# An attention block with Q and K projected transposed, V projected in one pass, and the sums turned through DRAM

## What is computed

```python
q = (X @ Wq), k = (X @ Wk), v = (X @ Wv)         # 16, 8, 8 heads of 64
q = q * cos + rotate_half(q) * sin; k likewise
att = 50 * tanh(q @ k.T / 16 / 50); causal; softmax
y = att @ v                                       # heads side by side, 1024 columns
x = layernorm(X + y @ Wo)
q8, s = int8 per token of x; ffn = (q8 @ weight.T) * s * w_scale + bias, to float16
out = layernorm(x + ffn)
```

## Time and profile before

| | us |
|---|---|
| median of 3 runs (1562.66 to 1565.54) | 1562.99 |
| span of the profiled execution | 1559.7 |
| start to the first score | 54.8 |
| a pair of attention | 36.1 |
| last weighing of a batch to the next tanh | 91.4 |
| TensorE, DVE, ACT, POOL busy | 1415.9, 1272.7, 986.5, 546.2 |

### The profile page before, as it was taken

How to read it: one execution, slowest core, us unless ns; L and a number is a source line. 1 busy time by engine, 2 the same in 40 slices (tenths; PEclk the granted TensorE clock), 3 DMA queues, 4 the chain that set the end, 5 groups by cost and what they waited for, 6 DMA issues and landing times.

```text
span 1559.7 us, 26316 instructions
## 1 busy us (share of the span) xinstructions
PE 1415.9 (91%) x8576; PEld 1141.8 (73%) x8576; DVE 1272.7 (82%) x3228; ACT 986.5 (63%) x1374; POOL 546.2 (35%) x529
## 2 busy tenths in 40 slices
PE   3699999989789999998969999998997999999894
PEld 3588878757678887866768788885776888888572
DVE  7888888867878888885788888887678888888575
ACT  5577777763367777784337777777335777777632
POOL 2433333333323333332433333333242333333434
PEclk9899999999989999999989999999999999999997
DMA  7300000311100000032110000002210000000211
GB/s 236 129 1 1 1 1 1 109 63 52 49 9 1 1 1 1 1 108 75 44 53 1 1 1 1 1 1 108 81 53 36 1 1 1 1 1 1 108 55 41
DMA packets 25337, 55.98 MB, mean 36 GB/s; under 512 B 3824, under 2 KB 12528, under 8 KB 23920
## 3 DMA queue, kind: packets, MB, share of 16 engines
q1 hardware_dynamic: 20592, 45.88, 8.6%
q10 hardware_dynamic: 4608, 8.39, 1.4%
...
## 4 chain that ended last, share of the span: by engine, by line
PE 58%; issue 12%; DVE 12%; ACT 11%; POOL 6%; DMA 0%; ACTq 0%; POOLq 0%; DVEq 0%; SPq 0%
PE ps L516 19%; PE ps L460 16%; PE ps L492 13%; PE ps L559 4%; ACT qkT L664 4%; ACT probs L677 4%; PE ps L526 3%; ACT sums L693 2%; POOL rstd L1048 1%; POOL f L1056 1%; DVE qkT L834 1%; DVE stats L938 1%; PE ps L476 1%; PE ps L477 1%; POOL prob_lo L1039 1%
## 5 line engine op out<-in xcount | busy, mean ns | idle before, releaser
L1039 POOL TENSOR_TENSOR prob_lo<-probs,prob_hi 128x1024 fp32r<-128x1024 f32 x128 | 310.8, 2428 | 559.6 <-DVE prob_hi L848 559.6
L460 PE MATMUL ps<-w_split,xT 128*128 128x256 f32 x3072 | 420.4, 288 | 30.2 <-DVE xT L788 22.3
L460 PEld LDWEIGHTS ps<-w_split,xT 128*128 128x128 f32 x3072 | 404.9, 195 | 48.1 <-issue 22.3
L516 PE MATMUL ps<-prob_hi,v 128*65 128x512 f32 (+3 forms) x1280 | 425.1, 381 | 13.8 <-POOL prob_lo L1039 12.0
L677 ACT ACTIVATE probs<-ps 128x1024 f32<-128x1024 f32 x288 | 295.4, 1026 | 160.9 <-PE ps L492 152.9
L492 PE MATMUL ps<-qkT 128*128 128x512 f32 (+1 forms) x1280 | 322.0, 378 | 14.9 <-DVE qkT L834 14.9
L683 ACT ACTIVATE probs<-probs 128x1024 f32<-128x1024 f32 x288 | 305.5, 1061 | 8.8
L492 PEld LDWEIGHTS ps<-qkT 128*128 128x128 f32 x1280 | 229.3, 193 | 73.8 <-DVE qkT L834 16.1
L664 ACT ACTIVATE qkT<-ps 64x256 fp32r<-64x256 f32 x512 | 193.5, 378 | 106.9 <-PE ps L477 101.6
L848 DVE CAST prob_hi<-probs 128x1024 fp32r<-128x1024 f32 x288 | 203.2, 706 | 54.1 <-POOL probs L1031 26.1
L834 DVE TENSOR_TENSOR qkT<-ps,qkT 64x256 fp32r<-64x256 f32 x512 | 215.1, 420 | 35.0 <-ACT qkT L664 26.8
...
## 6 DMA issues: line engine op xcount, KB each, us to landing
wo<-wo_split SPq DMA_DIRECT2D x8, 2048.0 KB, 7.5
...
x_in<-X SPq DMA_DIRECT2D x32, 256.0 KB, 3.1
result<-probs ACTq DMA_DIRECT2D x32, 256.0 KB, 2.0
wo_split<-y SPq DMA_DIRECT2D x2, 2048.0 KB, 7.3
...
y<-L_attn_Wo SPq DMA_DIRECT2D x1, 2048.0 KB, 10.4
y<-L_attn_Wk SPq DMA_DIRECT2D x4, 256.0 KB, 6.8
```

Of the source, the lines that this page charges most:

```text
L460: mm = nc.tensor.matmul(ps[:, proj_bank(j, t), 0:QKV], xT[:, a, k, rows], w_split[:, w, k, j, :], start=(k == 0 and a == w == 0), stop=(k ...
L516: mm = nc.tensor.matmul(sums_ps[:, :, GQ - n:GQ], v[:, j % 2, kt, w0:w1], p[:, g % ring, col:col + REP * n].rearrange("p (h q) -> p h q", ...
L1039: nc.gpsimd.tensor_tensor(prob_lo[:, g % PRING, :], probs[:, g % PRING, :], prob_hi[:, g % 2, :].bitcast(F32), ALU.subtract).then_inc(low_ ...
```

## The change

- **Units.** Four units of two pairs per batch (U = 16 in all, number m) take the place of pairs for the projection. Weights now stand on TensorE and tokens stream: a chunk is 128 output channels of all heads in a unit by up to 1024 columns, 24 matmuls of 512 columns. Unit m has chunk 0 (K, both halves of the tokens) and chunks 1 and 2 (Q, one half of the tokens each). They come out transposed, so `turn_qk`, `round_qk` and `split_qk` go. While unit m - 1 is in attention (18 steps), chunk 0 is projected in its steps 0 to 2, chunk 1 in 5 to 7, chunk 2 in 9 to 11, 8 matmuls each step. Also unit 0 of the next batch is projected beside the last unit of this one. The last unit of all has nothing beside it.
- **Rope.** Output channels are ordered so that the halves that rope exchanges lie in other partitions or columns. `rope_read` (DVE, out of PSUM, three passes for K, two for Q), `rotate` (POOL, adds and subtracts 1024 columns), `round_rope` (ACT) and `rope_low` (DVE) follow. SP puts the parts from the tile `work` to `qk` by DMA inside SBUF, 8 DMAs per chunk and part, 48 per unit.
- **V.** `project_v` makes V of all heads, 12 matmuls of 512 columns per token tile, once per batch; `round_v` (ACT) and `split_v` (DVE) split it. Tiles 0 to 4 come around the last two weighings of the batch before, 5 to 7 behind project_out(0).
- **Weights.** They are split at the start, unit by unit, by ACT and DVE or POOL in four stages that lie in other tiles, stored to DRAM (w_scratch) and loaded again for each unit. The rope tables are spread and turned once.
- **Sums.** `put_sums` stores unscaled sums (64 rows, rows of 512 B) and divisors of each group to DRAM in turned order, three DMAs. At the end of a batch the divisors are loaded into `div`, inverted, stored; ACT's queue loads them broadcast (`load_rb`, two DMAs per tile, one buffer), SP loads y; `scale_y` on POOL multiplies, `round_y` (ACT) and `split_y` (DVE) split. `turn_sums`, `finish_group` and `turn_y` go.
- **Order.** The loop over batches is unrolled in the program. The tail of the row phase stands alone before the next batch's scores.

The core of the diff (declarations, start and counts of semaphores are left out):

```diff
+                for i in range(2):
+                    if x == 0:
+                        for half in range(2):
+                            src = work_r[64 * half + 32 * i:64 * half + 32 * (i + 1), 0, 1 - low, :].bitcast(F32)
+                            for copy in range(2):
+                                r0 = 64 * copy + 32 * half
+                                sp.dma_start(buf[r0:r0 + 32, i, 2 + low, :].bitcast(F32), src
+                                             ).then_inc(k_put[m % 2][i], 16)
...
+                        for r in range(REP):
+                            h = REP * i + r
+                            for half in range(2):
+                                src = work_r[32 * h:32 * (h + 1), x, 1 - low, half * HT:(half + 1) * HT].bitcast(F32)
+                                r0 = 64 * low + 32 * half
+                                sp.dma_start(buf[r0:r0 + 32, i, r, cols].bitcast(F32), src
+                                             ).then_inc(q_put[m % 2][x - 1][i], 16)
...
+                for h in range(REP):
+                    sp.dma_start(y_scratch[2 * c:2 * c + 2, h * HD:(h + 1) * HD, j, :].rearrange("t d n -> d t n"),
+                                 sums[0:HD, slot, h * GQ:(h + 1) * GQ].rearrange("d (t n) -> d t n", t=2)
+                                 ).then_inc(sums_put[slot], 16)
+                sp.dma_start(d_scratch[2 * c:2 * c + 2, :, j, :].rearrange("t h n -> h t n").unsqueeze(0),
+                             sums[HD:HD + 1, slot, :].rearrange("a (h t n) -> a h t n", h=REP, t=2)
+                             ).then_inc(sums_put[slot], 16)
...
+                for slot in range(2):
+                    sp.wait_ge(sums_put[slot], sums_put_upto(b))
+                sp.dma_start(div[:, :], d_scratch.rearrange("t h j n -> (t h j) n")).then_inc(div_loaded, 16)
+                for x in range(1, 3):
+                    wait_put(sp, min(UB * b + UB, U - 1), x)
+                for t in range(YRING):
+                    load_y(b, t)
+                for t in range(XRING):
                     load_x(b, t)
...
+                sp.wait_ge(div_done, b + 1)
+                sp.dma_start(r_scratch.rearrange("t h j n -> (t h j) n"), div[:, :]).then_inc(div_stored, 16)
...
+                products = [(n, k, w, a) for n in range(2) for k in range(KC) for w, a in ((0, 0), (0, 1), (1, 0))]
+                for n, k, w, a in products[lo:hi]:
+                    half, slot = (n, 0) if x == 0 else (x - 1, 1 + n)
+                    mm = nc.tensor.matmul(ps[:, bank + n, :], w_ring[:, slot, w, k, :],
+                                          xT[:, a, k, half * HT:(half + 1) * HT],
+                                          start=(k == w == a == 0), stop=(k == KC - 1 and w == 1))
+                if hi == len(products):
+                    mm.then_inc(projected, 1)
...
+                        score(b, g)
+                        if m is not None:
+                            for x, at in enumerate((0, 5, 9)):
+                                if at <= s < at + 3:
+                                    project(m, x, 8 * (s - at), 8 * (s - at) + 8)
+                        if g >= 2:
+                            weigh(b, g - 2)
+                if more:
+                    project_v(b + 1, 0)
+                weigh(b, NB - 2)
+                if more:
+                    project_v(b + 1, 1)
+                weigh(b, NB - 1)
+                if more:
+                    for t in (2, 3, 4):
+                        project_v(b + 1, t)
+                for t in range(NT):
+                    if t == 1 and more:
+                        for n in (5, 6, 7):
+                            project_v(b + 1, n)
...
+            def load_rb(b, t):
+                if t == 0:
+                    act.wait_ge(div_stored, 16 * (b + 1))
+                    wait_put(act, min(UB * b + UB, U - 1), 0)
                 else:
...
+                    act.wait_ge(y_scaled, rows_upto(b, t - 1))
+                for h in range(REP):
+                    act.dma_start(rb[h * HD:(h + 1) * HD, :, :].rearrange("p k n -> p (k n)"),
+                                  r_scratch[t, h].rearrange("k n -> (k n)").partition_broadcast(HD)
+                                  ).then_inc(rb_loaded, 16)
...
+            def round_y(b, t):
+                act.wait_ge(y_scaled, rows_upto(b, t))
+                if t >= 2:
+                    act.wait_ge(o_done, rows_upto(b, t - 2))
+                elif t == 0:
+                    wait_put(act, min(UB * b + UB, U - 1), 1)
+                nc.scalar.activation(y_hi[:, t % 2, :, :], y_raw[:, t % YRING, :, :], ACT.Copy).then_inc(y_hi_done, 1)
...
+                        if m is not None and s in (5, 10, 14):
+                            round_rope(m, (5, 10, 14).index(s))
                         cap(b, g)
...
+                load_rb(b, 0)
+                load_rb(b, 1)
+                round_y(b, 0)
+                load_rb(b, 2)
+                round_y(b, 1)
+                if more:
+                    for t in range(5, NT):
+                        round_v(b + 1, t)
                 for t in range(1, NT):
+                    if t + 2 < NT:
+                        load_rb(b, t + 2)
                     if t + 1 < NT:
...
+                        round_y(b, t + 1)
...
+                if x == 0:
+                    cos_k, sin_k = (table[:, :].rearrange("p (a c) -> p a c", a=2) for table in (cosT, sinT))
+                    nc.vector.tensor_tensor(turned, halves, cos_k, ALU.mult)
+                    nc.vector.scalar_tensor_tensor(out=crossed[0:HD], in0=halves[HD:P], scalar=-1.0, in1=sin_k[0:HD],
+                                                   op0=ALU.mult, op1=ALU.mult)
+                    nc.vector.tensor_tensor(crossed[HD:P], halves[0:HD], sin_k[HD:P], ALU.mult).then_inc(proj_read, 1)
+                else:
+                    cols = slice((x - 1) * HT, x * HT)
+                    swapped = bass.AP(tensor=halves.tensor, offset=halves.offset + 512,
+                                      ap=[[8 * 512, P], [-512, 2], [1, 512]])
+                    cos_q, sin_q = (table[:, cols].unsqueeze(1).broadcast_to([P, 2, HT]) for table in (cosT, sinT))
+                    nc.vector.tensor_tensor(turned, halves, cos_q, ALU.mult)
+                    nc.vector.tensor_tensor(crossed, swapped, sin_q, ALU.mult).then_inc(proj_read, 1)
+            def rope_low(m, x):
+                dve.wait_ge(rope_hi, chunks_upto(m, x))
+                nc.vector.tensor_tensor(work_r[:, x, 0, :], work[:, x, 0, :], work_r[:, x, 1, :].bitcast(F32),
...
+                        if m is not None and s in (3, 8, 12):
+                            rope_read(m, (3, 8, 12).index(s))
+                        if g >= 1:
+                            probs_of(b, g - 1)
+                        if m is not None and s in (6, 11, 15):
+                            rope_low(m, (6, 11, 15).index(s))
...
+            def rotate(m, x):
+                pool.wait_ge(proj_read, chunks_upto(m, x))
+                pool.sem_inc(wait_passed, 1)
+                if x == 0:
+                    nc.gpsimd.tensor_tensor(work[:, 0, 0, :], work[:, 0, 0, :], work[:, 0, 1, :],
+                                            ALU.add).then_inc(rotated, 1)
...
+                        mask(b, g)
+                        if m is not None and s in (4, 9, 13):
+                            rotate(m, (4, 9, 13).index(s))
...
+            def scale_y(b, t):
+                pool.wait_ge(y_loaded[t % YRING], ring_upto(b, t, YRING))
+                pool.wait_ge(rb_loaded, 32 * rows_upto(b, t))
+                nc.gpsimd.tensor_tensor(y_raw[:, t % YRING, :, :], y_raw[:, t % YRING, :, :], rb[:, :, :],
+                                        ALU.mult).then_inc(y_scaled, 1)
...
+                scale_y(b, 0)
+                scale_y(b, 1)
+                for t in range(1, NT):
+                    inverse_std(b, t - 1, 0, mv1, veps1, rstd1, z_done)
+                    if t + 1 < NT:
+                        scale_y(b, t + 1)
```

1121 lines of the change are left out of this document (632 added, 489 removed).

## The result

The changed kernel takes 1832.71 us (median of 4, 1830.25 to 1833.75) beside 1562.83 for the kernel before on the same chip: a ratio of 1.172, 95% interval 1.171 to 1.174, slower by 17%. The prediction was 1661 with a range of 1575 to 1720: the direction was right, the size far outside.

A forecast was written before the change was run, and what follows sets the result against it. Attention was taken as TensorE-bound. Start 78, attention 279.8 + 2 x 274.8 + 250, handoffs 3 x 125.5 and end 124 gave a span of 1658 us, 1661 as run; range 1575 to 1720.

The forecast's parts named there:

- the chain: Attention, score to weighing on the other engines: 4.5 to 5.7 us a group against TensorE's 4.6, with rope passes queued ahead.
- The first rival: Attention: TensorE paces the units, 59 us each, since engine queues recover within a unit; 1541 us in all; 12 in 100.
- where projection products follow they cover the delay: stalls 1.1 us at step 4, 0.5 at step 7: Attention unit: products in steps 5 to 7 and 9 to 11 hide rope delays; only the third chunk lacks cover, 3.9 us.
- the size of rotate: POOL's rope additions and subtractions in attention: 2.43 us per chunk, like a low part, three times per unit.
- the collision of POOL and DVE: Attention: each of three rotates can hold DVE, a cast taking 1.82 us instead of 0.7; adds 2.4 us a unit.
- The split of x: End of a batch's attention: falls into the bare steps of unit 2 and costs 3.5 us.
- SP has room: SP's queue in attention: 48 puts at some 0.35 us, 17 of 67 us per unit, and 8 more for sums.
- The third rival: Attention and handoff: puts and broadcasts land late, 2 us more a unit and 6 a handoff, 1715 us; 17 in 100.
- Handoff: Last weighing to next batch: sums through DRAM in series, project_out(0) at 18.8 us, next score at 125.5; 105 lost over three.
- SP issues five loads meanwhile: Handoff: five loads issued during the 0.5 us reciprocal, given no cost of their own; the store after it 2.4 us.
- The loop of 12.9: Row phase: period rises from 8.46 to 12.9 us through scale_y, two issues, round_y, keep_q and norm1, less split_y.
- The start: Before the first score: weight loads, splits, stores, K rope and puts; first score at 78 us, 23 lost, bounds 68 and 92.

## Why the prediction was right or wrong

**Right: that the direction is decided by the chain, not by TensorE.** Without its waits TensorE needs some 61 of the second unit's 72.7 us (forecast 59), and the unit didn't follow. The first rival (60.5 or less a unit) fell: even without rotate a unit takes 61 to 65.

**Wrong: "where projection products follow they cover the delay: stalls 1.1 us at step 4, 0.5 at step 7".** This is the step that failed: in the unit shown above the waits outside the third chunk are 7.3 us, not 1.6. Two things were missing in it. I had ACT waiting for rotate ahead of the tanh at the third chunk only, where I counted 3.9 and 4.35 came. The same order acts at all three chunks, with 3.5 to 5.8 us of standstill on ACT each, and the products of one step (8 times 0.234, 1.9 us) don't cover that. Moving the rounding alone gave back 74 us; attention was under-forecast by 114. And the size of rotate: 2.43 was taken from a low part, but for Q it is two passes that DVE's casts and low parts interrupt, 3.5 us in the mean (1769 and 1730 ns). One pass gave back 19. How far the two gains overlap was not tried. With rotate away altogether attention takes 1072 us in sum over the batches, where 1075 was forecast with it: the forecast fits a kernel without rotate.

**Mis-sized: the collision of POOL and DVE.** The prediction had the row, a cast of 1.82, and priced it at 2.4 a unit, then took 67 because terms overlap. Casts take up to 2.89 and rose by 444 ns in the mean, which is 8 us over the 18 casts of a unit, not all of it on the path. The Trainium skill, SBUF — State Buffer, Who interferes with whom, has the shared port pair as an exclusive lock: the engine that issues first holds it for its whole instruction, and the other is blocked. The rows of split_y (3.29 beside a pass of 2.40 that began 0.20 before) agree with this; in the units, where both engines keep issuing, POOL's passes get longer too (1.27 to 2.26 for 512 columns).

**Third unit.** The split of x was put at 3.5 and cost 4.7: the third unit takes 78.5 with it and 73.8 in batch 3, which has none. ACT waits for its load (16.1 us in all, 36.3 with the rounding moved), and the load goes out 13 us behind the end of the projection, since it stands behind the puts of chunk 1. A term of transfer was missing; I had costed only the engines' passes.

**Right in part: the puts.** TensorE's waits for Q and K's puts are 28.8 us: 26.0 ahead of the first score, 2.9 in the first unit and none later, so the puts themselves land in time. But they cost SP 0.62 each, not 0.35, and "SP has room" left out what stands behind them: the load of x in each third unit, and the first score. The third rival, late puts, has next to nothing for it in attention; in the handoff it was partly true.

**Handoff: 126.5 against 140.** Of the 13.4 us, 4.4 come before the first projection: the store of the reciprocals takes 6.0 instead of the 2.4 taken from the result's store at 2.0. It is issued right behind three loads of y and two of x, which the working passed over with "SP issues five loads meanwhile"; no run takes these loads away, so that they are what delays it is likely, not shown. Another 1.5 come until residual1(1) ends (46.4 against 40.5), the rows give 6.6 (76.8 against 70.2; 3.7 of it at tile 2, 14.8 where 11.1 was forecast, and 11.6 with the weights late and V first) and the tail 1. The Trainium skill, DMA: Bandwidth & Descriptors, Anatomy of one DMA, has about 2.0 us fixed a transfer; its section is written for transfers that GpSimd issues, and all of these are issued by SP or ACT. The divisors' load at 1.7 and the puts at 2.0 to 2.3 are near it all the same; the store at 6.0 and the broadcasts at 4.0 are not, and the measurement decides.

**Rows: mechanism right, another loop longer.** The loop of 12.9 exists: the run with keep_q first has it at 12.9 to 13.3. I wrote that TensorE's own work falls and "so it waits", and didn't ask what it waits for: keep_q behind round_y, and residual1 behind TensorE at its lower clock. That loop is 13.7 long. Without the division the period was 8.5, not the 10.2 that I expected from my sum: round_y then waits for nothing in the loop, so all that was put in goes with scale_y, not its own passes alone.

**Start and end.** The start took 84.4 against 79. The engines were in time there: K's chunk is rounded at 62.2, near the 64 of the forecast, but the first score comes at 82.3, 20 us later where 14 were meant, at the end of a wait for the puts, which SP issues one behind the other. The end's 10.5 is the handoff's miss again.
